# One reduction over two PSUM banks: row maxima of four heads together in an attention and mixture-of-experts kernel

## The reference

```
xn = layernorm(layernorm(x)) * gamma + beta
q = (xn @ Wq + bq) in 8 heads of 16;  k likewise;  v in 8 heads of 128
scores = q . k / sqrt(16);  p = softmax(scores);  att = p @ v
out = att.reshape(S, B, D, H).sum(-1)           # x = x + out
gates = sigmoid(u @ centroids.T), the best 2 of 8 kept and normalised
h = gelu(u @ W1[e] + b1[e]);  outs = h @ W2[e] + b2[e]
out = sum over e of gates[:, e] * outs[e]       # x = x + out
```

## Time and profile before

| | us |
|---|---|
| median of 3 runs | 740.27 |
| lowest and highest | 736.64, 744.0 |
| profiled execution | 735.11 |
| its span, first to last instruction | 733.3 |
| TensorE busy in the span | 597.0 (81%) |
| VectorE busy in the span | 540.1 (74%) |
| ScalarE, GpSimd busy | 461.1, 417.6 |

### The profile page before, as it was taken

The page is one execution under the profiler, slowest core; times in us unless marked ns, Lnnn a source line. Parts: engine busy times, 40 slices in busy tenths (PEclk is TensorE's granted clock), DMA queues, the critical chain, the costliest instruction groups (busy, mean ns, idle before and its releaser), DMA issues.

```text
span 733.3 us, 14671 instructions
## 1 busy us (share of the span) xinstructions
PE 597.0 (81%) x3993; PEld 448.8 (61%) x3993; DVE 540.1 (74%) x1588; ACT 461.1 (63%) x872; POOL 417.6 (57%) x467
## 2 busy tenths in 40 slices
PE   8799998888988889988867573878999999999300
PEld 7566666565666566666546462767877777877200
DVE  6789899898889989889646462656776776767364
ACT  3367876676766776765668552766787777778100
POOL 5223347667677667767773745545565566556700
PEclk9999999999999999999888877999999999999855
DMA  5655544455454454443174534897876777775089
GB/s 135 176 137 148 144 140 128 129 167 165 125 146 129 136 167 144 136 137 113 51 206 136 185 113 122 221 268 203 248 217 221 231 222 216 241 251 193 16 358 328
DMA packets 107570, 127.33 MB, mean 174 GB/s; under 512 B 19949, under 2 KB 86009, under 8 KB 106496
## 3 DMA queue, kind: packets, MB, share of 16 engines
q1 hardware_dynamic: 89600, 105.34, 48.8%
q0 software_dynamic: 9088, 16.94, 7.6%
q10 hardware_dynamic: 8832, 4.46, 2.1%
HBM read 69.26 MB, written 33.72 MB: 140 GB/s over the span
## 4 chain that ended last, share of the span: by engine, by line
PE 16%; issue 9%; SPq 7%; DMA 6%; DVE 4%; ACT 4%; POOL 3%; another core or an unknown queue 2%; POOLq 0%; DVEq 0%; ACTq 0%
DMA probs<-comb 3%; PE ps_max L999 2%; PE ps_max L1001 2%; PE ps_max L1000 2%; PE ps_route L1050 2%; ACT k_stack L798 2%; DMA probs<-slots 1%; POOL slots L602 1%; PE ps_proj L1058 1%; SPq L392 1%; PE ps_st L1001 1%; PE ps_st L999 1%; SPq L401 1%; PE ps_st L1000 1%
## 5 line engine op out<-in xcount | busy, mean ns | idle before, releaser
L672 POOL DMA_INDIRECT comb<-probs,gate_row x156 | 157.8, 1011 | 107.1 <-issue 41.4
L699 ACT ACTIVATE probs<-ps_st 128x512 f32<-128x512 f32 x256 | 146.3, 592 | 92.2 <-PE ps_st L860 84.6
L1089 DVE TENSOR_REDUCE row_max<-ps_max 128x2 f32<-128x512 f32 x256 | 172.8, 682 | 32.6 <-PE ps_max L848 29.5
L602 POOL DMA_INDIRECT slots<-y_row,slot_idx x128 | 126.7, 990 | 65.6 <-issue 43.4
L1358 DVE TENSOR_TENSOR k_stack<-probs,k_stack 128x512 fp32r<-128x512 f32 x156 | 107.7, 690 | 74.6 <-ACT k_stack L798 56.5
L848 PE MATMUL ps_max<-k_stack,q_stack 96*128 96x256 f32 x512 | 128.7, 334 | 32.3 <-DVE row_max L1089 24.1
L848 PEld LDWEIGHTS ps_max<-k_stack,q_stack 96*128 96x128 f32 x512 | 78.8, 190 | 82.0 <-DVE row_max L1089 43.5
L860 PE MATMUL ps_st<-q_stack,k_stack 128*128 128x256 f32 x512 | 107.3, 292 | 4.4 <-ACT probs L699 2.1
L860 PEld LDWEIGHTS ps_st<-q_stack,k_stack 128*128 128x128 f32 x512 | 79.7, 192 | 12.4 <-ACT probs L699 7.2
L795 ACT ACTIVATE probs<-ps_st,b_cur 128x512 f32<-128x512 f32 x78 | 54.4, 698 | 33.6 <-DMA b_cur<-b_all 13.9
L878 PE MATMUL ps_av<-probs,v_aug 128*32 128x256 f32 x1024 | 69.8, 391 | 0.0
(11 more groups left out here) (179 smaller groups left out, 1243.5 us busy)
## 6 DMA issues: line engine op xcount, KB each, us to landing
q_stack<-w_split SPq DMA_DIRECT2D x78, 512.0 KB
probs<-slots SPq DMA_DIRECT2D x39, 260.0 KB
q_stack<-q_hi SPq DMA_DIRECT2D x64, 128.0 KB
k_stack<-k_hi SPq DMA_DIRECT2D x64, 128.0 KB
probs<-comb SPq DMA_DIRECT2D x8, 1024.0 KB, 7.9
X<-in_L_attn_x_dram SPq DMA_DIRECT2D x16, 256.0 KB
q_stack<-q_lo SPq DMA_DIRECT2D x32, 128.0 KB
k_stack<-k_lo SPq DMA_DIRECT2D x32, 128.0 KB
```

The costliest lines, as they stand in the source:

```text
L602: pool.indirect_dma_start(slots, bass.IndirectOffsetOnAxis(slot_idx[par_s][:, k, c:c + 1], 0), y_row[par_s][k][:, c, :], None).then_inc(sc ...
L672: pool.indirect_dma_start(comb_rows, bass.IndirectOffsetOnAxis(gate_row[r][:, c, 1:2].bitcast(I32), 0), res[r][:, c * P:(c + 1) * P], None ...
L699: act.activation(probs[slot % 2][:, h, :, :], ps_st[h % 2][:], ACT.Exp, scale=DK ** -0.5).then_inc(exp_done, 1)
L1089: dve.tensor_reduce(row_max[slot % 2][:, sc, 2 * hp:2 * hp + 2], ps_max[k % 2][:], AX.X, ALU.max).then_inc(smax_reduced, 1)
```

## The change

The two PSUM tensors `ps_max[0]` and `ps_max[1]` become one tensor `ps_max4` of four times 256 numbers, that is two neighbouring banks. TensorE makes the matmuls of units k and k + 1 (k even) directly after one another, ahead of `st_unit` k; it waits once for the pair, until all earlier units are reduced. VectorE reduces once for each odd k: one operation over both banks gives the maxima of four heads and adds 2 to `smax_reduced`. At even k VectorE has no reduction any more, so that the work of an even k follows directly on the work of the odd k before it. `st_unit` and all else keep their k. The second stage uses halves of `ps_max4` as it used the two tensors.

```diff
-        ps_max = [ctx.enter_context(nc.psum_tensor(f"ps_max{n}", [P, 2, S], F32)) for n in range(2)]
+        ps_max4 = ctx.enter_context(nc.psum_tensor("ps_max4", [P, 4, S], F32))
...
-        ps_o = [ps_max[n][:].rearrange("p a s -> p (a s)") for n in range(2)]
+        ps_o = [ps_max4[:, 2 * n:2 * n + 2, :].rearrange("p a s -> p (a s)") for n in range(2)]
...
                     sc, hp = k // 4, k % 4
-                    wait(pe, smax_reduced, 8 * b + k - 1)
+                    if k % 2 == 0:
+                        wait(pe, smax_reduced, 8 * b + k)
                     for hh in range(2):
                         h = 2 * hp + hh
-                        last = pe.matmul(ps_max[k % 2][:, hh, :], q_stack[slot][0:M_ROW, h, sc * P:(sc + 1) * P],
+                        last = pe.matmul(ps_max4[:, 2 * (k % 2) + hh, :], q_stack[slot][0:M_ROW, h, sc * P:(sc + 1) * P],
                                          k_stack[slot][0:M_ROW, h, :], start=True, stop=True)
                     last.then_inc(smax_ready, 1)
...
                 for k in units:
-                    max_unit(t, k)
+                    if k % 2 == 0:
+                        max_unit(t, k)
+                        max_unit(t, k + 1)
                     st_unit(t, k)
...
             def reduce_unit(t, k):
                 nb = t.batch(0)
-                if nb:
+                if nb and k % 2 == 1:
                     b, bi, slot = nb
-                    if k == 0:
+                    if k == 1:
                         wait(dve, maxT_ready, b - 1)
                     sc, hp = k // 4, k % 4
                     wait(dve, smax_ready, 8 * b + k + 1)
-                    dve.tensor_reduce(row_max[slot % 2][:, sc, 2 * hp:2 * hp + 2], ps_max[k % 2][:], AX.X,
-                                      ALU.max).then_inc(smax_reduced, 1)
+                    dve.tensor_reduce(row_max[slot % 2][:, sc, 2 * hp - 2:2 * hp + 2], ps_max4[:], AX.X,
+                                      ALU.max).then_inc(smax_reduced, 2)
```

## The result

| | before | after |
|---|---|---|
| median of 4 runs, us | 739.89 | 764.5 |
| lowest and highest | 736.64, 744.0 | 761.3, 766.65 |
| profiled execution, its span | 735.11, 733.3 | 766.65, 764.9 |
| VectorE, TensorE busy in the span | 540.1, 597.0 | 532.5, 608.6 |
| mean granted TensorE clock | 0.933 | 0.909 |

The ratio is 1.0344, with a 95% interval of 1.0285 to 1.0404. The forecast of 746 us leaned to the right side and its range, up to 759, doesn't hold the result.

What follows compares the result with a forecast made beforehand. TensorE and VectorE were both near 90% busy, neither bounding alone. Early batches +4, first two batches +3, late periods -5 and clock +4 summed to +6 us on the 740.3 median: 746 us, range 733 to 759.

Steps and rivals of the forecast that it cites:

- The long reduction: On VectorE, one reduction of 1024 numbers takes 1.21 us; 128 pairs save 13 us of VectorE time, bounds 0 and 19.
- the rival that it would take as long as two: Long reduction takes 1.36 us or more, so nothing is saved: +10 us, 750 us, chance 0.13.
- The loop of 2.05 us: Between units 0 and 2, TensorE waits for four matmuls, their signal, the 1.21 us reduction and a signal back.
- Batches 2 to 9, +4: Early attention periods: each two periods grow from 18.05 to 19.1 us, four times, +4 us, bounds +1 and +7.
- First two batches, +3: Start of the attention stage, where no scores cover the loop: +3 us, bounds +1 and +6.
- Late even periods, -0.75: Even periods where VectorE also places tokens: next period starts near 167.4 in place of 168.16, a gain of 0.75 us.
- Late odd periods, +0.25: Late odd periods lose 0.25 us each by the early ones' argument; with late even ones, -5 us over ten pairs.
- the last sentence of the prediction: The forecast is wrong if TensorE's late signal moves with the new order; its time was taken as given.
- The bound of +1.4: Upper bound for a late odd period, if TensorE's signal for the pair comes only 2.3 us after unit 0.
- The clock, +4: Longer TensorE idling before unit 2 lowers its clock: 0.9 us in four of ten places, +4 us, bounds 0 and +9.
- The clock rival: Idle before unit 2 exceeds about 1.5 us, so the clock falls each late even period: +17, 757 us, chance 0.25.
- The relief rival: VectorE is the engine behind and its relief reaches the end: -5 to -12, taken as 732 us, chance 0.17.

Runs made afterwards that it cites:

- e8: The kernel before, with SyncE's wait before the transfers that place the q and k stacks put three units later: 695.94 us, 1.0012 of the kernel before.
- c_after_2: The changed kernel again, unchanged, beside a faster level of the kernel before: 728.15 us against 695.01, 1.0439.
- c_after: The changed kernel profiled again, unchanged: 759.5 us against 736.36 for the kernel before, 1.0327.
- c_before: The kernel before profiled again, unchanged: 736.8 us in one run.
- e1: The kernel before, with the matmuls of two units made together and its short reductions and waits kept: 720.71 us against 692.1, 1.0407.
- e5: The changed kernel, with the long reduction at even k, right after the work of k - 1: 751.47 us against 736.36 for the kernel before, 1.0208.
- e12: The kernel before, with GpSimd's second half of scatters after the addition to X: 728.58 us against 735.45, 0.9895.
- e11: The changed kernel, with the long reduction at even k and, in even periods, units 2 and 3 just before the products with v: 752.33 us, 1.0183 of the kernel before.
- e13: The changed kernel, with GpSimd's second half of scatters after the addition to X: 730.8 us against 695.21 for the kernel before, 1.0488.

## Why the prediction was wrong

**The long reduction: right in its length, too high in what it saves.** It took 1.221 us where 1.21 was forecast, so the rival that it would take as long as two is out. (That rival's price was not the sum of its terms either: 5 for the loops and 1.5 for ten gains at unit 7 on top of the +6 give 12 or 13, 752 or 753 us, and not 750.) VectorE's busy time was to fall by 10 to 13 us and fell by 7.6, of which 5.6 are picked alone, which got shorter for another reason (the last section). At the lower level, where picked is short in both kernels, it fell by 3.3 (538.1 in e8, 534.8 in c_after_2). So the sum had too much on the side of the saving as well.

**The loop of 2.05 us: right.** In the early odd period of batch 5 unit 2 starts 2.13 us after unit 0 (forecast about 2), in the even one of batch 6 it is 2.66 (about 2.5), in a late even one 2.97 (about 3). TensorE's rows of the changed kernel, batches 5 to 7 (the earlier trace rows before):

```profile
70.83 0.71 PE L849 MATMUL ps_max<-k_stack,q_stack 96*128 96x256 f32 x4
...
72.96 0.74 PE L849 MATMUL ps_max<-k_stack,q_stack 96*128 96x256 f32 x4 [0.72 <-DVE row_max L1092]
...
79.93 0.71 PE L849 MATMUL ps_max<-k_stack,q_stack 96*128 96x256 f32 x4
...
82.59 0.74 PE L849 MATMUL ps_max<-k_stack,q_stack 96*128 96x256 f32 x4 [1.26 <-DVE row_max L1092]
...
90.25 0.71 PE L849 MATMUL ps_max<-k_stack,q_stack 96*128 96x256 f32 x4
```

**Batches 2 to 9, +4: too small.** The pair of batches 5 and 6 takes 19.42 us in place of 18.05, +1.37 where +1.05 was forecast. But not every pair is like it. In c_after against c_before, batch by batch from 2 to 9: +2.7, +0.4, +1.0, +0.3, +1.0, +1.1, +0.3, +1.05, together +7.9. Batch 2 has 6.8 us at half clock in it. Batches 7 and 9, odd ones, lose 1.1 each and not 0.2: they are the first odd ones in which experts are chosen, and batch 7 of the changed kernel has units 2, 4 and 6 where the late odd ones below have them (2.12, 5.15 and 7.84 us after unit 0, where before had 2.10, 4.68 and 6.44). The upper bound of this term was +7.

**First two batches, +3: about right in the first pair** (+2.5). The second pair (-0.5) can't tell, with 14 us at half clock in c_before's 19.1.

**Late even periods, -0.75: right in its course, too large as a gain, and lost to the clock in part.** Where the clock held they take 11.02 in place of 11.50 and 11.03 in place of 11.44, and the forecast had 11.0. In batch 22 units 2, 4 and 6 and the next period start 2.88, 6.10, 8.72 and 11.01 us after unit 0, where the forecast had 3.1, 6.55, 8.85 and 11.05. The gain is 0.4 to 0.5 and not 0.75, since it was reckoned from one of the longer periods (11.81). And it is one of the upper level: at the lower, where the kernel before has neither late signals nor a long picked, the same periods lose 0.35 (10.62 in e8, 10.97 in c_after_2 with the clock at 1.00).

**Late odd periods, +0.25: the step that failed.** It read "Odd late periods lose 0.25 by the same argument as the early ones", and gave +1.4 as a bound. They lost 1.81 (before and after), 1.67 (c_before, c_after) and, at the lower level, 0.95 (9.96 in e8, 10.91 in c_after_2); against +0.25 that is 14.0 and 12.8 us over nine periods in the first two, their falls of the clock included: most of the 18.5 us by which the median missed. Two mechanisms stand in it, and the falls come on top. An estimate from these means: the first is 0.95 us a period, which the lower level shows without late signals and falls; the second adds what the upper level loses beyond it with the clock at 1.00 (1.49 and 1.08), 0.1 to 0.5; the falls are the rest, 0.3 to 0.6.

The first is the work of the choice of experts, which the early odd periods that I read (batch 5) don't have. It shows cleanly at the lower level. VectorE in an odd period of c_after_2:

```profile
183.46 1.23 DVE L1092 TENSOR_REDUCE row_max<-ps_max 128x4 f32<-128x1024 f32 x1 [0.91 <-PE ps_max L849]
184.62 0.87 DVE L1237 BATCH_NORM_STATS2 bn<-X 128x6 f32 x4
186.37 0.19 DVE L1115 TENSOR_TENSOR den<-expn,ones 128x32 f32<-128x32 f32 x1 [0.88 <-ACT expn L737]
186.53 1.23 DVE L1092 TENSOR_REDUCE row_max<-ps_max 128x4 f32<-128x1024 f32 x1
187.67 0.34 DVE L1118 RECIPROCAL sig<-den 128x32 f32<-128x32 f32 x1
188.22 0.72 DVE L1206 STREAM_TRANSPOSE att<-ps_av 128x512 f32<-128x512 f32 x1 [0.21 <-DVE sig L1118]
188.86 0.33 DVE L1121 MAX8 top<-sig 128x8 f32<-128x8 f32 x4
189.38 1.23 DVE L1092 TENSOR_REDUCE row_max<-ps_max 128x4 f32<-128x1024 f32 x1 [0.19 <-DVE top L1121]
```

And TensorE in the same period, units 0, 2, 4, 6 and the next 0:

```profile
182.61 0.74 PE L849 MATMUL ps_max<-k_stack,q_stack 96*128 96x256 f32 x4
...
184.74 0.74 PE L849 MATMUL ps_max<-k_stack,q_stack 96*128 96x256 f32 x4
...
187.81 0.74 PE L849 MATMUL ps_max<-k_stack,q_stack 96*128 96x256 f32 x4 [0.23 <-issue]
...
190.66 0.74 PE L849 MATMUL ps_max<-k_stack,q_stack 96*128 96x256 f32 x4 [0.78 <-DVE row_max L1092]
...
193.64 0.74 PE L849 MATMUL ps_max<-k_stack,q_stack 96*128 96x256 f32 x4 [0.75 <-DVE row_max L1092]
```

The matmuls of units 2 and 3 start at 184.74 and can be reduced some 0.85 us later, as those of units 0 and 1 are. The reduction starts at 186.53: bn_stats stand ahead of it, and then den, which waits 0.88 us for ScalarE's exponential of the logits. Before, unit 2 was reduced ahead of den and TensorE could make unit 4. The next reduction stands behind sig, the transpose and max8, at 189.38, and unit 6 waits for it until 190.66. Counted from unit 0, units 2, 4, 6 and the next period start at 2.13, 5.2, 8.05 and 11.03 us; at the same level the kernel before (e8) had 2.08, 4.67, 6.51 and 9.88. Next to nothing is lost at the first loop, which was the one I had worked out; 0.5 is lost at the second and 1.0 more at the third, of which 0.4 come back by the next period. e1 has the matmuls of a pair together and short reductions in their old places, and loses nothing in odd periods; e5, which puts the long reductions ahead of these operations again, brings the odd periods to 10.74, from 11.79.

The second is that TensorE's late signal moves with the new order, as the last sentence of the prediction feared. At the upper level, the changed kernel, an odd period, TensorE and then VectorE:

```profile
184.43 0.74 PE L849 MATMUL ps_max<-k_stack,q_stack 96*128 96x256 f32 x4
...
187.75 0.74 PE L849 MATMUL ps_max<-k_stack,q_stack 96*128 96x256 f32 x4 [0.98 <-DVE row_max L1092]
```

```profile
186.47 1.22 DVE L1092 TENSOR_REDUCE row_max<-ps_max 128x4 f32<-128x1024 f32 x1 [2.09 <-PE ps_max L849]
```

VectorE idled 2.09 us until the signal came 2.04 after the start of the matmuls, and unit 2 started 3.32 after unit 0 in place of 2.13. In this trace it starts about 2 us after unit 0 in the odd periods 13 to 23, and 0.95 in the later ones. In the kernel before, the first reduction starts 1.44 after unit 0 in the odd periods 17 to 23, and 2.17 in period 15, so that the trace of before had a case of it. The bound of +1.4 had this very case, "if TensorE's signal for the pair comes only 2.3 us after unit 0". With the bound in place of the value ten odd periods give +14 for +2.5: the sum would have been +17.5 in place of +6, and the time 757 or 758.

**The clock, +4: within its bounds, made up otherwise.** In batches 12 to 29 the clock fell 10 times after and once before, 7 times and 3 times in the second pair, nearly always for 3.4 us. A fall costs an even period 1.6 us (11.01 and 12.58 in c_after_2), and an odd one 0.6 (12.00, the only one of the odd periods 13 to 23 without a fall, and 12.6 in after), where 0.9 was taken. That is 4 even falls for 1 and 6 odd ones more, 3 x 1.6 + 6 x 0.6 or about 8 us, in the first pair, and 4 odd ones more, 2.4 us, in the second. The clock rival (757) came nearest to the time, and its sign came true (0.93 in 140 to 340 us, below 0.97), but its reason didn't. TensorE idles 1.44 or 1.53 us in one piece before unit 2 in every even period from 12 to 22 of after, and the clock fell in two of these six; five of its falls are in the odd periods of that stretch, where the piece is 0.9 to 1.2. With the falls removed by fillers in the even periods the kernel still was at 1.027.

**The relief rival is out.** VectorE's lower load passed nothing on: it idles more than before in the same 200 us (41.4 us, 21.1 before).

## What to carry to other kernels

Two banks that alternate are a hand-over with one unit of slack; one operation over both is the same work with none, and the 0.03 to 0.06 us of VectorE's time that a pair saved here (3.3 and 7.6 us over 128) don't pay for it (1.03 to 1.04 times the time, and 1.11 for the wait alone). Before merging two operations of an engine in order, list everything that stands between them in every kind of period, with its waits for third engines: what stood between them goes ahead of the merged one, and the partner waits for all of it. A term's upper bound whose condition the trace already shows (a first reduction 1.8 us after unit 0 in the late even period, 2.17 in an odd one) should be weighed as a case, and not left as a bound.

## What the runs showed of the hardware

TensorE's signals can be late by two microseconds. In the traces at the upper level the semaphore updates behind the products with v at the end of a period come up to 2.2 us after the end of the last matmul (before, odd to even; 0.6 even to odd), and VectorE's first reduction of the next period starts later by a part of that (1.9 us after unit 0 in c_before's even periods, 1.33 in e12's; 0.7 to 1.6 and 0.55 to 0.6 in odd ones). Up to batch 8, before the scatters begin, the delay is 0.04 us in the same traces. With GpSimd's second half of scatters moved behind the addition to X it was 0.04 us throughout (e12), at the same level; in e5 and e11, also at that level and with the scatters in their old place, it was 0.04 at the end of even periods and 0.04 to 2.6 at the end of odd ones. At the lower level it was 0.04 with the scatters in either place (c_after_2, e1, e8, e13). What holds the signal is therefore not the scatters alone, and stays open.

The two levels themselves are unexplained. From the lower to the upper level the kernel before loses 24 to 27 us in the second stage (336.6 us in e8, 360.7 and 363.9 in c_before and before) and 12 to 17 us ahead of it. The change costs less at the upper level, for a reason that the periods show: there the kernel before pays for the late signal, and for what the next paragraph tells, in its even periods (11.44 with the clock at 1.00, 10.62 in e8), which the changed one, with bn_stats and picked ahead of its reduction, doesn't (11.03 and 10.97).

The even periods of the kernel before have a second burden at the upper level, and it lies on GpSimd. picked, a VectorE operation on 32 numbers, took 1.26 us in the earlier trace rows; GpSimd's product bv_raw had started just before it:

```profile
159.50 1.27 POOL L567 TENSOR_TENSOR bv_raw<-Wv_raw,ones_e 128x512 fp32r<-128x512 f32 x1
```

In all eight even periods from batch 10 to 24 it is so, in before as in c_before: bv_raw starts up to 0.3 us ahead of picked, picked takes 0.8 to 1.3 us, and it ends 0.05 us after bv_raw does. In e8, e12 and after the two don't meet in these periods, and picked takes 0.17 us in each:

```profile
198.34 0.17 DVE L1140 TENSOR_TENSOR picked<-chosen 128x32 bf16<-128x32 f32 x1
```

So the same operation is five to seven times as long beside another engine's, and that is gone in these three kernels (in e5 it takes 0.3 to 0.7). The rank matmuls wait for picked, so a part of what late even periods gain in the changed kernel, and in e12, is this and not the hand-over; how large a part no run here tells.
